# Displacing the places of the rounded weights modulo 512 bytes in a three-part decoder layer

## What is computed

```python
x = _layernorm(x + mamba(x), axis=-1)                  # input projection, conv, scan, output projection
x = _layernorm(x + cross_attention(x, ctx), axis=-1)   # 16 heads, 4 key/value heads, 1536 keys
x = _layernorm(x + feed_forward(x), axis=-1)           # silu(x W1') * (x W3') W2'
# mamba:  proj = hidden_states @ in_proj_w             (1024 tokens x 1024) @ (1024 x 4096)
# feed_forward: w = wq * w_scale, blocks of 128 x 128
g = xf @ dequant(w1).T ; u = xf @ dequant(w3).T        # 1024 -> 3584
y = (silu(g) * u) @ dequant(w2).T                      # 3584 -> 1024
```

## Time and profile before

| what | us |
|---|---|
| median of 2 timed runs | 3048.39 |
| lowest and highest | 3046.60, 3050.18 |
| span of the profiled execution | 3047.5 |
| PE busy | 2833.3 |
| DVE busy | 2393.1 |
| POOL busy | 1712.8 |
| ACT busy | 1574.6 |

### The profile page before, as it was taken

The page is one execution under the profiler, slowest core; times in us unless marked ns, Lnnn a source line. Parts: engine busy times, 40 slices in busy tenths (PEclk is TensorE's granted clock), DMA queues, the critical chain, the costliest instruction groups (busy, mean ns, idle before and its releaser), DMA issues. The chain is left out here.

```text
span 3047.5 us, 35696 instructions
## 1 busy us (share of the span) xinstructions
PE 2833.3 (93%) x11958; PEld 2028.4 (67%) x11958; DVE 2393.1 (79%) x2168; ACT 1574.6 (52%) x2685; POOL 1712.8 (56%) x1035
## 2 busy tenths in 40 slices
PE   8997588888788889999999999999989999999997
PEld 7882244444222348888888888887768888887886
DVE  6558999999999977444777777765988888885677
ACT  4448555555665545213888888873433333334443
POOL 0003999999999953403888888861044444430034
PEclk9995799999999999999999999999989999999999
DMA  4228886666875645232111111215245555567654
GB/s 152 83 83 261 274 200 159 179 171 152 250 219 148 199 150 216 104 119 72 37 37 37 37 37 37 71 54 200 97 156 180 180 179 180 180 218 238 194 176 139
DMA packets 217641, 445.84 MB, mean 146 GB/s; under 512 B 33661, under 2 KB 47741, under 8 KB 215613
## 3 DMA queue, kind: packets, MB, share of 16 engines
q1 hardware_dynamic: 179742, 390.73, 41.1%
q10 hardware_dynamic: 37728, 52.96, 5.3%
HBM read 313.45 MB, written 130.15 MB: 146 GB/s over the span
## 5 line engine op out<-in xcount | busy, mean ns | idle before, releaser
L1927 POOL TENSOR_TENSOR at_p_lo<-at_p,at_p_hi 128x512 fp32r<-128x512 f32 x384 | 514.6, 1348 | 244.3 <-ACT at_p_hi L1820 236.5
L716 POOL TENSOR_TENSOR scan_dbx<-scan_u,scan_b_bc 128x1024 f32<-128x1024 f32 x256 | 596.1, 2359 | 0.0
L885 ACT ACTIVATE mamba_ps<-scan_dt,scan_a_neg 128x512 f32<-128x512 f32 (+1 forms) x512 | 332.0, 680 | 315.1 <-DVE scan_g L903 291.3
L914 DVE TENSOR_TENSOR_SCAN mamba_ps<-mamba_ps,scan_dbx 128x1024 f32<-128x1024 f32 x195 | 440.0, 2283 | 3.1 <-ACT mamba_ps L887 1.7
L1847 DVE TENSOR_REDUCE at_neg_max<-heads_ps 128x1 fp32r<-128x1536 f32 x128 | 224.9, 1757 | 134.4 <-PE heads_ps L1939 132.4
L108 PE MATMUL heads_ps<-ff_x_hi,ff_w_hi 128*128 128x512 f32 x784 | 310.0, 395 | 17.2 <-DVE ff_u L2572 6.4
L2812 POOL TENSOR_TENSOR ff_raw<-ff_raw,ff_scale 128x512 f32<-128x512 f32 x112 | 115.9, 1066 | 361.2 <-DMA ff_raw<-in_w 252.8
L109 PE MATMUL heads_ps<-ff_x_lo,ff_w_hi 128*128 128x512 f32 x784 | 308.1, 393 | 0.0
L110 PE MATMUL heads_ps<-ff_x_hi,ff_w_lo 128*128 128x512 f32 x784 | 308.1, 393 | 0.0
L1816 ACT ACTIVATE at_p<-heads_ps 128x512 f32<-128x512 f32 x384 | 228.2, 594 | 110.0 <-PE heads_ps L1963 95.8
L1820 ACT ACTIVATE at_p_hi<-at_p 128x512 fp32r<-128x512 f32 x384 | 242.8, 632 | 12.2
(11 more groups left out here) (306 smaller groups left out, 6906.8 us busy)
## 6 DMA issues: line engine op xcount, KB each, us to landing
scan_dt<-dt SPq DMA_DIRECT2D x120, 256.0 KB, 4.8
scan_u<-u SPq DMA_DIRECT2D x120, 256.0 KB, 7.6
ff_raw<-in_w SPq DMA_DIRECT2D x56, 512.0 KB, 4.6
ff_down_ar<-ac SPq DMA_DIRECT2D x98, 256.0 KB, 2.8
ff_down_hr<-hc SPq DMA_DIRECT2D x98, 256.0 KB, 2.7
ff_act_w<-in_w SPq DMA_DIRECT2D x14, 1024.0 KB, 7.6
hc<-ff_act_t SPq DMA_DIRECT2D x56, 256.0 KB, 6.2
ac<-ff_act_v SPq DMA_DIRECT2D x56, 256.0 KB, 5.9
```

Source lines behind the costliest of these rows:

```text
L716: nc.gpsimd.tensor_tensor(dbx[n % SL][:].rearrange("p (h l) -> p h l", h=2), u[it % 2][:, c:c + 2], b_bc[b][:, k // 2].unsqueeze(1).to_bro ...
L885: nc.scalar.activation(at[:, h * L + h:(h + 1) * L], dt[it % 2][:, c, h:L], ACT.Exp, scale=a_neg[:, it % IT, e:e + 1]).then_inc(a_ready, 1)
L914: nc.vector.tensor_tensor_scan(out[:], ps_a[n % SA], dbx[n % SL][:], 0.0, ALU.mult, ALU.add).then_inc(scanned, 1)
L1927: nc.gpsimd.tensor_tensor(p_lo[n % NSL][:], p[n % NSL][:], f32(p_hi[n % NSL][:]), ALU.subtract).then_inc(p_lo_done, 1)
```

## The change

The ring of the feed-forward part gets 32 bytes of space after each of its sixteen places, so that `w_hi0` has residue 0, `w_lo0` 32, `w_hi1` 64, `w_lo1` 96 and so on to `w_lo7` with 480. After the ring the arena is aligned again: all tiles behind it (`p0`, `u2` to `u4`, `raw`, the scales) lie 512 bytes further and keep their residue. The same holds for the arena `ff_wo`, which lies over the last place. In the input projection the four places get 64 spare bytes each, and the tile that is used starts 16, 48, 4 or 8 bytes into its place. The residues become 16 (`w_hi0`), 112 (`w_lo0`), 132 (`w_hi1`) and 200 (`w_lo1`), and the order in memory is now hi, lo, hi, lo. All tiles of the input projection behind them lie 256 bytes further. `xc_hi`, `xc_lo` and `xpw_hi`, `xpw_lo` move together, so that the distances between them stay.

```diff
@@ mamba_in
-    w_hi = [sb(f"w_hi{s}", [P, HT, P], F32R) for s in range(2)]
-    w_lo = [sb(f"w_lo{s}", [P, HT, P], F32R) for s in range(2)]
+    w_hi, w_lo = [], []
+    for s in range(2):
+        for part, name, by in ((w_hi, "w_hi", (16, 4)[s]), (w_lo, "w_lo", (48, 8)[s])):
+            wide = sb(f"{name}{s}", [P, HT * P + 16], F32R)
+            part.append(wide[:, by // 4:by // 4 + HT * P].rearrange("p (k m) -> p k m", m=P))
@@ attention_out_feed_forward
+    STEP = 32
@@
         if s == NW - 1:
-            wo_at = Arena(nc, "ff_wo", sb.at)
+            wo_at = Arena(nc, "ff_wo", sb.at).align()
         w_hi.append(sb(f"w_hi{s}", [P, HK, P], F32R))
+        sb.at += STEP
         w_lo.append(sb(f"w_lo{s}", [P, HK, P], F32R))
+        sb.at += STEP
+    sb.align()
```

## The result

The changed kernel takes 3074.64 us (median of 2 runs, 3074.26 to 3075.02), the one before 3048.39 us. The ratio is 1.0083, with a 95% interval of 1.0054 to 1.0113. The kernel became slower by 26.2 us, where 17 us was forecast. The profiled execution spans 3073.7 us, which is also 26.2 us more than before.

What follows compares the result with a forecast made beforehand. PE's matmul stream was taken to bound the input, up- and down-projection. Terms of 9.4 + 5.1 + 3.7 = 18.2 us on 3047.5 gave 3065.7, timed 3066 to 3067, less 2 for settling: 3065 us, range 3033 to 3092.

Steps and rivals of the forecast that it cites:

- what bounds the stages: Input, up- and down-projection: PE's matmul pace is the time; in the norm stretch VectorE's work covers 191 matmuls, counting nothing.
- an interval of 0.2265 us is a settled pace that displacement gives up: Matmul stream at full clock: 0.2265 us, 0.0133 us above bare, holds with equal residues and no disturbance; displaced weights lose it.
- writers and waits: ScalarE's rounding and VectorE's subtraction: displaced outputs could cost 3.4 us, hidden by idle time; no waits added.
- the mean interval: Three stages: mean rises from 0.2265 to 0.2308 us, ends 0.223 and 0.237; adds 9.4, 5.1 and 3.7 us.
- the swallowing that the prediction left out: Up- and down-projection: PE's 7.4 us of waits could absorb a little of the loss; not counted.
- the row behind the 0.2308 us: An `xproj` with displaced operands: 13 intervals in 3.00 us, 0.2308 us each, taken as the new mean.
- the jumps: Feed-forward ring: weight loads jump 32 bytes twice in three matmuls, so the settled pace of 0.2265 us gives way to 0.2308 us.
- 2 us off for settling part of the way: Whole sum: some products of 12 matmuls settle part of the way, which takes 2 us off.
- The pattern: Ring: if addresses matter, intervals depend on the ring slot and repeat every 8 products.
- Only timing counts: Rival for the matmul stream: addresses don't matter, the settled interval stays 0.2265 us, time 3048; chance 0.14.
- The distance frees the stream: Rival, 4219 matmuls: reads apart stop interfering, down to 0.2133 us, -55.7 us, 2992 us; chance 0.08 in part, 0.05 wholly.
- The reads exclude each other: Rival, 4219 matmuls: both reads in turn, 0.2667 us, +169.6 us, 3218 us; called remote; any mean above 0.237 us has 0.07.

Runs made afterwards that it cites:

- the map: Ring and input-projection places set at many distances from the moving operand, against the kernel before: single runs of 3070.35, 3070.77, 3068.96, 3071.22 and 3068.18 us.

## Why the prediction was right

**Right: what bounds the stages.** The forecast rested on PE's pace being the time in three stages and not in the stretch of the norms. The stage lengths after the change differ by 6.3, 12.7 and 5.7 us. In the stretch of the norms the 192nd matmul of the up-projection starts 76.6 us after the first one before, and 76.4 us after it with the change.

**Right: an interval of 0.2265 us is a settled pace that displacement gives up.** The distance in address is what changes it. Runs at one constant distance of 32 bytes (+25.2 us), of 256 bytes (0.2268 us in the ring) and with both operands moved (0.2267 us) show this directly.

**Right: writers and waits.** The displaced outputs cost the writers nothing. The groups of the changed kernel that answer to the earlier trace rows (count, busy us, mean ns, idle before):

```profile
L2384 ACT ACTIVATE ff_w_hi<-heads_ps 128x512 fp32r<-128x512 f32 x112 | 66.9, 597 | 178.0 <-DVE heads_ps L2568 152.8 <-PE heads_ps L110 25.1
L2573 DVE TENSOR_TENSOR ff_w_lo<-heads_ps,ff_w_hi 128x512 fp32r<-128x512 f32 x112 | 77.0, 688 | 41.1 <-ACT ff_w_hi L2384 39.4
```

That is 597 ns after 598 and 688 after 687.

The prediction's count of the writes is low (the ring is rounded 294 times, 112 + 84 + 98, and not 210), which changes nothing, since the price was none.

**Mis-sized: the mean interval.** The step that took 0.2308 us from the earlier trace rows as the new mean was the term too small. Over all intervals under 250 ns the means rose from 226.8 to 232.6 ns in the up-projection and the down-projection, and from 227.2 to 233.0 ns in the input projection. With the forecast's counts, 2179 x 0.0059 + 1176 x 0.0058 + 864 x 0.0059 = 24.8 us, of 26.2 us measured. By stage this is 12.9, 6.8 and 5.1 us, against 12.7, 5.7 and 6.3 us measured. The down-projection has 1.1 us less, of which 0.7 us are PE's shorter waits (6.7 in place of 7.4 us), the swallowing that the prediction left out. The input projection has 1.2 us more, its longer opening at 0.427 us.

**Luck: the row behind the 0.2308 us.** The earlier trace rows show a stream on its way back to the cheap pace. The earlier trace rows was taken because its addresses differ. But it doesn't show a price of distance. It is an `xproj` of slot 1, with a distance of 128 bytes at every load. The next `xproj`, of slot 0, has distances of 256 and 0 bytes, which cost a settled stream nothing. Its first matmul and the one 13 intervals later, in the kernel before:

```profile
33.22 0.39 PE L108 MATMUL mamba_ps<-in_xc_hi,in_xpw_hi 128*96 128x512 f32 x1
...
36.21 0.39 PE L109 MATMUL mamba_ps<-in_x_lo,in_w_hi 128*128 128x512 f32 x1
```

That is 2.99 us, against 3.00 us in the earlier trace rows. The unrounded starts give 2.987 and 2.994 us, 229.8 and 230.3 ns an interval. So 3.1 of the 3.6 ns above the cheap pace are there without any distance modulo 256. Both have the same six matmuls with 96 columns to load in the stream, and the disturbance most likely comes with them. That a passing disturbance of 3 to 4 ns lies within a factor of two of the lasting 6 ns of displacement is luck, and so is a part of the forecast's nearness.

**Wrong: the jumps.** The prediction gave the steps of 32 bytes between successive weight loads as what unsettles the ring. One constant distance without any jump in the ring costs as much (0.2333 us), and jumps of 256 bytes cost nothing (0.2268 us).

**Wrong: 2 us off for settling part of the way.** It did settle, mostly within 4 to 12 matmuls, but to cycles of its own at 231 to 233 ns. Settled is not the same as cheap.

**Wrong in detail.** The pattern was expected to repeat every 8 products. It repeats every 4, since the period in address is 256 bytes and not 512.

**The rivals.** "Only timing counts" fell with the constant distance of 32 bytes. "The distance frees the stream" fell with the map: no distance gives less than 226.7 ns, let alone 213.3. "The reads exclude each other" (266.7 ns) never appeared, and the longest single interval in the ring is 241 ns. By the rule of the Trainium skill's page "SBUF — State Buffer", section "Who interferes with whom", that TensorE's two read ports are independent and that it never waits on anyone, addresses would change nothing. These traces don't agree, and the measurement decides: the same instructions at the same clock, with nothing waited for, need 226.7 or 233.3 ns by address alone. The 518 cycles that the Trainium skill's page "TensorE: Matmul & The Clock Gate", section "Back-to-back issue gap", gives for 512 columns are 215.8 ns, and no settled stream of these matmuls reached them.

## What to carry to other kernels

Where PE bounds a stage with a stream of fp32r matmuls at a granted clock of 1.00, read its pace from the starts in the timeline, and not from busy times. Then compare it between stages or slots: a difference of some ns with a strict period points to addresses. Give the stationary and the moving operand the same address modulo 256 bytes, in every slot of a ring, and keep the stream uniform in width. Here that is worth some 25 us of 3075, for less than 512 bytes of padding at each `align()`. Only 512 moving columns of fp32r were seen to gain; with 384 moving columns a distance of 32 bytes made no difference.

## What the runs showed of the hardware that I had not expected

- At 2.4 GHz a matmul with 512 moving fp32r columns and a weight load of 128 columns has a pace of 226.7 to 235.4 ns when settled, by distance in address and in steps as fine as 4 bytes, with a period of 256 bytes. At 1.2 GHz it has 426.7 ns, at every distance that fell into such a stretch (among them 0, 32, 96 and 128 bytes).
- A settled stream needn't be even. It may run in a cycle of 2, 3, 7 or more intervals (at 96 bytes 232, 237, 238, 231, 234, 235, 233 ns and again), to 1 ns over many matmuls.
- With 384 moving columns 32 bytes of distance cost nothing: 173.3 ns, 13.3 ns above the bare columns, like the 13.3 ns of 512 columns at distance 0.
- The same input projection ran at 0.427 us an interval until 11.1 us in one execution and until 13.8 us in another. A difference of 1 us between two kernels at this place says nothing.
- Halving the columns that ten of twelve matmuls load and use made the stream slower at distance 0 (229.5 against 226.7 ns). Which two accesses meet in SBUF, and why the extra of the best pace is 13.3 ns, stays open.
